# A local-attention and FFN stack on one core: the remainders of x on GpSimd, the maxima ahead of the FFN's gates, the rotary sines and the softmax division in one VectorE operation each

## The reference

```python
def attn_layer(x, Wqkv, qs, ksc, Wo):          # 16 heads of 64, windows of 32 tokens
    q, k, v = split(x @ Wqkv)
    q = l2norm(q) * qs;  k = l2norm(k) * ksc
    q = q * cos * scale + rotate_half(q) * sin * scale
    k = k * cos / scale + rotate_half(k) * sin / scale
    out = local_attention(q, k, v)             # own window and the one before it, softmax
    return out @ Wo

def ffn_layer(x, g, bln, W1, b1, W2, b2):
    xn = (x - mean(x)) / sqrt(var(x) + 1e-05) * g + bln
    a, gate = split(xn @ W1 + b1)
    return a * gelu(gate) @ W2 + b2

for i in range(6):
    x = attn_layer(shift_tokens(x), ...) + x
    x = ffn_layer(shift_tokens(x), ...) + x
```

## Time and profile before

| what | value |
|---|---|
| time, median of 3 runs | 3898.07 us (3895.68 to 3901.53) |
| the profiled execution's own time | 3892.5 us |
| its span in the trace | 3890.7 us |
| PE busy | 3564.2 us, 92% |
| DVE busy | 3275.5 us, 84% |
| POOL busy | 2781.9 us, 72% |
| ACT busy | 2617.8 us, 67% |
| mean granted clock of PE | 0.986 of full |
| DMA engines, mean busy over the span, queue of the data | 28.8% |

### The profile page before, as it was taken

The page is one execution under the profiler, slowest core; times in us unless marked ns, Lnnn a source line. Parts: engine busy times, 40 slices in busy tenths (PEclk is TensorE's granted clock), DMA queues, the critical chain, the costliest instruction groups (busy, mean ns, idle before and its releaser), DMA issues. The chain is left out here.

```text
span 3890.7 us, 104815 instructions
## 1 busy us (share of the span) xinstructions
PE 3564.2 (92%) x38876; PEld 2641.0 (68%) x38876; DVE 3275.5 (84%) x4930; ACT 2617.8 (67%) x3817; POOL 2781.9 (72%) x2428
## 2 busy tenths in 40 slices
PE   5888889699999999999999999999999999999995
PEld 4666666476777776776767676767676767777772
DVE  5656665499999999998999999999899999999993
ACT  3555555377777777777777777777777777777773
POOL 2444443288888787878787878788888888787871
PEclk9999999899999999999999999999999999999997
DMA  1122221232324232233332343222432324232221
GB/s 49 71 81 80 93 75 44 70 79 65 69 64 116 65 72 65 65 87 94 70 69 64 70 111 72 65 65 66 112 74 64 69 64 115 65 72 65 65 66 54
DMA packets 181947, 285.96 MB, mean 73 GB/s; under 512 B 52222, under 2 KB 71804, under 8 KB 175612
## 3 DMA queue, kind: packets, MB, share of 16 engines
q1 hardware_dynamic: 181884, 285.14, 28.8%
HBM read 51.11 MB, written 32.51 MB: 21 GB/s over the span
## 5 line engine op out<-in xcount | busy, mean ns | idle before, releaser
L442 PE MATMUL st_ps<-st_wqkv,st_xs 128*128 128x512 f32 x4608 | 1266.6, 410 | 47.2 <-issue 20.1
L828 POOL TENSOR_TENSOR st_qk_rot<-st_qk_rot,st_qk_sq 128x1024 f32<-128x1024 f32 x384 | 913.7, 2385 | 506.0 <-DVE st_qk_sq L728 506.0
L442 PEld LDWEIGHTS st_ps<-st_wqkv,st_xs 128*128 128x128 f32 x4608 | 811.8, 189 | 285.0 <-issue 143.5
L848 POOL TENSOR_TENSOR st_qk_rot<-st_qk_rot,st_rn 128x1024 f32<-128x1024 f32 x384 | 731.5, 1926 | 15.0
L710 DVE TENSOR_REDUCE st_nt<-st_qk_sq 128x16 f32<-128x1024 f32 x384 | 466.0, 1214 | 66.1 <-ACT st_qk_sq L559 50.1
L728 DVE TENSOR_TENSOR st_qk_sq<-st_ps,st_rot 128x512 f32<-128x512 f32 x768 | 490.5, 679 | 0.0
L714 DVE TENSOR_TENSOR st_qk_rot<-st_ps,st_rot 128x1024 f32<-128x1024 f32 x384 | 468.7, 1220 | 7.5 <-PE st_ps L457 1.6
L1525 DVE TENSOR_REDUCE at_nmx<-at_s 128x1 f32<-128x512 f32 (+3 forms) x512 | 237.0, 487 | 246.1 <-PE at_s L1138 244.8
L457 PE MATMUL st_ps<-consts_sb,st_qk_rot 128*128 128x128 f32 x3072 | 402.2, 274 | 28.9 <-POOL st_qk_rot L848 24.6
L457 PEld LDWEIGHTS st_ps<-consts_sb,st_qk_rot 128*128 128x128 f32 x3072 | 352.4, 141 | 106.5 <-issue 67.9
L877 POOL TENSOR_TENSOR st_s<-st_s,st_mx 128x512 f32<-128x512 f32 x384 | 403.6, 1071 | 10.2 <-DVE st_mx L783 9.8
(11 more groups left out here) (149 smaller groups left out, 6167.7 us busy)
## 6 DMA issues: line engine op xcount, KB each, us to landing
st_v_win<-st_v_tok SPq DMA_DIRECT2D x3072, 64.0 KB, 2.0
st_wqkv<-wqkv_parts SPq DMA_DIRECT2D x24, 1024.0 KB, 7.1
wqkv_parts<-at_w_parts SPq DMA_DIRECT2D x12, 1024.0 KB, 4.4
wqkv_parts<-at_fold_parts SPq DMA_DIRECT2D x12, 1024.0 KB, 4.7
at_w_raw<-in_wqkv SPq DMA_DIRECT2D x18, 512.0 KB, 5.5
at_wo_l<-in_wo SPq DMA_DIRECT2D x6, 512.0 KB, 5.8
rotary_tables<-at_rot SPq DMA_DIRECT2D x6, 512.0 KB, 4.7
st_rot<-rotary_tables SPq DMA_DIRECT2D x24, 128.0 KB, 2.5
```

The source lines that it names most:

```text
L442: last = pe.matmul(out[:, c * 512:(c + 1) * 512], xs[:, x_part, t * P:(t + 1) * P], wqkv[:, PROJ.index(kind), w_part, c * 512:(c + 1) * 51 ...
L828: pool.tensor_tensor(qk_rot[:, cols], qk_rot[:, cols], qk_sq[:, cols], ALU.add).then_inc(rot_done[a], 1)
L848: pool.tensor_tensor(view, view, rn[:, par, heads_of(a)].unsqueeze(2).to_broadcast([P, HEADS, DH]), ALU.mult).then_inc(normed[a], 1)
```

## The change

Four edits, all in `local_stack`:

- `remainder_half` for the running stack moves from VectorE to GpSimd. The second half of the running unit moves from the end of VectorE's tile 0 to the start of GpSimd's tile 1, ahead of the FFN's five operations. The first half of the next unit moves from VectorE's tile 2 to the start of GpSimd's tile 3. The two remainders before unit 0 stay on VectorE.
- In tile 1 the maxima of the scores stand in front of `gate(0)` and `gate(1)` on VectorE, where they stood between `gate(1)` and `gate(2)`.
- The multiplication by the sines is one operation of 1024 elements for q and one for k. It reads the halves of each head in reversed order, by a step of -32 elements.
- The division is one operation of 1024 elements. For it the inverse sums are written twice each, so `reciprocal` has 32 elements where it had 16.

```diff
-                            for g in range(2):
-                                sines = rot[:, t, 1, a * DH + g * (DH // 2):a * DH + (g + 1) * (DH // 2)]
-                                last = dve.tensor_tensor(dst[:, :, g, :], src[:, :, 1 - g, :],
-                                                         sines.unsqueeze(1).to_broadcast([P, HEADS, DH // 2]), ALU.mult)
-                            last.then_inc(rot_read[a], 1)
+                            sines = rot[:, t, 1, a * DH:(a + 1) * DH].rearrange("p (g d) -> p g d", g=2)
+                            dve.tensor_tensor(dst, src[:, :, ::-1, :], sines.unsqueeze(1).to_broadcast([P, HEADS, 2, DH // 2]),
+                                              ALU.mult).then_inc(rot_read[a], 1)
...
-                            dve.reciprocal(den[:, t2 % 2, 1, :], den[:, t2 % 2, 0, :]).then_inc(den_ready, 1)
+                            dve.reciprocal(rden[:, t2 % 2, :].rearrange("p (b s h) -> p b s h", b=2, s=2),
+                                           den[:, t2 % 2, :].rearrange("p (b h) -> p b h", b=2).unsqueeze(2)
+                                           .to_broadcast([P, 2, 2, HEADS // 2])).then_inc(den_ready, 1)
                             dve.wait_ge(den_ready, 2 * (n - 2))
-                            for b in range(2):
-                                last = dve.tensor_tensor(bank_of(s[:, t2 % 2, :], b), bank_of(weights, b),
-                                                         per_head(den[:, t2 % 2, 1, :], b), ALU.mult)
-                            last.then_inc(taken["ex"], 1)
-                        if t == 1 and alive(u, -2):
-                            gate(0)
-                            gate(1)
+                            dve.tensor_tensor(s[:, t2 % 2, :].rearrange("p (x k) -> p x k", k=WIN),
+                                              weights.rearrange("p (x k) -> p x k", k=WIN),
+                                              rden[:, t2 % 2, :].unsqueeze(2).to_broadcast([P, 2 * HEADS, WIN]),
+                                              ALU.mult).then_inc(taken["ex"], 1)
...
                             last.then_inc(max_ready, 1)
-                        if t == 2 and alive(u, 1):
-                            remainder_half(u, 1, 0)
                         if t == 1 and alive(u, -2):
+                            gate(0)
+                            gate(1)
                             gate(2)
...
-                        if t == 0 and alive(u, 0) and alive(u, -1):
-                            remainder_half(u, 0, 1)
...
             @block.gpsimd
             def _(pool):
+
+                def remainder_half(u, d, half):
+
+                    pool.wait_ge(xs_high, halves_done(u, d, half))
+                    cols = slice(half * 2 * P, (half + 1) * 2 * P)
+                    pool.tensor_tensor(xs[:, 1, cols], columns_of(batch_of(u, d), half * 2 * P, 2 * P),
+                                       xs[:, 0, cols].bitcast(F32), ALU.subtract).then_inc(xs_ready, 1)
...
+                        if t == 1 and alive(u, 0) and alive(u, -1):
+                            remainder_half(u, 0, 1)
+                        if t == 3 and alive(u, 1):
+                            remainder_half(u, 1, 0)
                         if t == 1 and alive(u, -2):
```

More of the change, by code:

```diff
@@ L249, in local_stack @@
         mx = sb("mx", [P, 2, HEADS])
-        den = sb("den", [P, 2, 2, HEADS])
+        den = sb("den", [P, 2, HEADS])
+        rden = sb("rden", [P, 2, 2 * HEADS])
         probT = sb("probT", [P, INNER])
@@ L759, in unit @@
                             for b in range(2):
-                                last = dve.tensor_reduce(den[:, t2 % 2, 0, b * 8:b * 8 + 8], heads_first(weights, b), AX.XY, ALU.add)
+                                last = dve.tensor_reduce(den[:, t2 % 2, b * 8:b * 8 + 8], heads_first(weights, b), AX.XY, ALU.add)
                             last.then_inc(den_ready, 1)
                             dve.wait_ge(den_ready, 2 * (n - 2) - 1)
-                            dve.reciprocal(den[:, t2 % 2, 1, :], den[:, t2 % 2, 0, :]).then_inc(den_ready, 1)
+                            dve.reciprocal(rden[:, t2 % 2, :].rearrange("p (b s h) -> p b s h", b=2, s=2),
+                                           den[:, t2 % 2, :].rearrange("p (b h) -> p b h", b=2).unsqueeze(2)
+                                           .to_broadcast([P, 2, 2, HEADS // 2])).then_inc(den_ready, 1)
                             dve.wait_ge(den_ready, 2 * (n - 2))
-                            for b in range(2):
-                                last = dve.tensor_tensor(bank_of(s[:, t2 % 2, :], b), bank_of(weights, b),
-                                                         per_head(den[:, t2 % 2, 1, :], b), ALU.mult)
-                            last.then_inc(taken["ex"], 1)
-                        if t == 1 and alive(u, -2):
-                            gate(0)
-                            gate(1)
+                            dve.tensor_tensor(s[:, t2 % 2, :].rearrange("p (x k) -> p x k", k=WIN),
+                                              weights.rearrange("p (x k) -> p x k", k=WIN),
+                                              rden[:, t2 % 2, :].unsqueeze(2).to_broadcast([P, 2 * HEADS, WIN]),
+                                              ALU.mult).then_inc(taken["ex"], 1)
                         if t == 3 and alive(u, -1):
```

## The result

| | before | after |
|---|---|---|
| time, median (lowest to highest) | 3897.5 us (3895.68 to 3901.53), 4 runs | 3864.12 us (3860.27 to 3868.4), 4 runs |
| ratio, 95% interval | 1 | 0.9909 [0.9895, 0.9923] |
| profiled execution, its span | 3892.5, 3890.7 us | 3860.27, 3858.5 us |
| DVE, POOL, PE busy | 3275.5, 2781.9, 3564.2 us | 3148.2, 2824.5, 3565.7 us |

The changed kernel is 0.9% faster, 33 us by the medians. The forecast was 3858 us in a range of 3842 to 3882.

What follows compares the result with a forecast made beforehand. PE was taken as nearly the bound, with waits before `pt` and `h` to win. 0.73 + 0.06 + 0.07 + 0.06 = 0.92 us a unit, 42 us over 46 units, taken as 40: 3858 us, range 3842 to 3882.

Steps and rivals of the forecast that it cites:

- The bound: Loop: PE nearly the bound at 95% busy; the chain from `q` to `pt` sets time in three of four tiles.
- Tile 1 at `pt`: Tile 1: L710 starts 0.68 us earlier without L681, merged sines save 0.06; `pt` moves forward 0.74 us.
- Tile 1 at `h`: Tile 1, FFN's `h`: L626 waits for the later of GpSimd's chain and ACT, coming 0.73 us earlier.
- Tile 2: Tile 2: `pt` gains the merged sines' 0.06 us; moving the maxima is worth 0.
- Tile 3: Tile 3: 0.07 us from the remainder no longer holding L795, plus 0.06 us from the sines.
- The changes of layer: Units that also wait for weights may give less: 40 us taken in place of 42.
- The slower rival: L728's reversed PSUM read is dear: with d = 0.5 us, +1.6 us a unit, 3970 us; chance 0.07.
- The rival with the whole fixed part: Each merged operation saves 0.14 us, 0.08 more, at four places: 0.3 us a unit, 3843 us; chance 0.07.
- The slower engine: Remainder goes to GpSimd, slower at it: 0.73 us by the line, against VectorE held 1.98 us there.
- The rival in which GpSimd is late in tile 1: Tile 1: remainder costs 1.04 us, unit gains 0.58, 3871 us; L721 missing a gap too, 3885; chance 0.15.
- Division and maxima: Division with reciprocal about 0 together; maxima worth 0, covered in tile 2 by L710's wait for the squares.
- The other signs: Expected: reciprocal 0.35 us, L877 2.06, tile 1's `pt` wait 0.2, L626 within 0.1 of GpSimd, unit 62.9 us.

Runs made afterwards that it cites:

- the two experiments that moved `h` alone: Changed kernel with GpSimd's tile 1 remainder behind the FFN's five operations: ratio to before 0.9881; changed kernel with an extra unused subtraction ahead of that remainder: 0.9985.
- the remainders alone: Kernel before with one edit, both remainders on GpSimd at the starts of its tiles 1 and 3: ratio 0.9952, median 3879.33 us.
- the remainder behind the FFN: Changed kernel with GpSimd's remainder of tile 1 behind the FFN's five operations instead of ahead: ratio to before 0.9881, median 3851.75 us.
- the sines alone: Kernel before with one edit, the sines in one operation for q and one for k: ratio 0.9966, median 3883.52 us.
- the division alone: Kernel before with one edit, division in one operation and reciprocal on 32 elements: ratio 0.9995, median 3898.4 us.
- the maxima alone: Kernel before with one edit, the maxima of tile 1 ahead of the gates: ratio 0.9997, median 3898.55 us.
- the second execution of the changed kernel: The changed kernel, unaltered, run again for direct comparison on one chip: ratio to before 0.9921, median 3866.31 us.
- twice: Changed kernel with an extra, unused subtraction of the same size ahead of GpSimd's remainder in tile 1: ratio to before 0.9985, median 3895.92 us.

## Why the prediction was right

**The bound** was read rightly. PE's waits before `pt` and `h` were what could be won, and the two experiments that moved `h` alone moved the unit by the same amount, 0.43 us one way and 0.64 the other. The time came out 6 us above the forecast, since the unit gained 0.73 us in the mean and not 0.92. Below, a tile's numbers are those of the unit shown.

**Tile 1 at `pt`.** Forecast 0.74 us, measured 15.06 - 14.32 = 0.74; the remainders alone gave 0.68. The wait is 0.29 rather than 0.22.

**Tile 1 at `h`.** Forecast 0.73, measured 21.64 - 21.06 = 0.58. GpSimd's chain ended 19.74 us after tile 0's `pt`, and the forecast's 2160.37 is 19.75 after it. That the two agree is luck, for two terms were off and cancel: L884 (before, L877) starts 0.06 us earlier after tile 0's `pt` than it did (10.99 against 11.05), not 0.16, and the remainder moves what follows by 0.59, not 0.70. What was mis-sized is the step from there to ACT: I let L626 start 0.05 us after GpSimd's end, and it starts 0.20 after it, here and with the remainder behind the FFN. That is the 0.15. In the units with the longer remainder, which moves what follows by the forecast's 0.70, `h` gains 0.48 only, and the mean over all is 0.52. L721 was forecast to end near 2157.8, 17.2 after `pt` of tile 0; as L722 it ended at 2144.35, 17.16 after it.

**Tile 2** gave 0.06 more, as forecast (34.08 - 33.44 = 0.64 in all). **Tile 3** was to give 0.07 by the missing remainder and 0.06 by the sines, and gave 0.07 together. The first of these did not come, and the reading behind it was wrong. L793, once L795, waits for `zt` with nothing ahead of it, 0.62 us; the rows are `zt` before, `zt` after and L793:

```profile
2183.73 0.27 PE L451 MATMUL st_ps<-consts_sb,st_z_tok 128*128 128x128 f32 x1
2169.65 0.27 PE L452 MATMUL st_ps<-consts_sb,st_z_tok 128*128 128x128 f32 x1
2170.07 0.59 DVE L793 TENSOR_TENSOR xT_sb<-st_ps,xT_sb 64x128 f32 x2 [0.62 <-PE st_ps L452]
```

It starts 0.15 us after `zt` ends (2169.92 to 2170.07). Before, L795 started 0.15 us after `zt` ended as well (2184.00 to 2184.15), so it was `zt`, and not the remainder ahead of it, that held it.

**Between tile 3 and the next tile 0** came 0.07 that was not forecast. `tq` there waited for GpSimd's L848, and started 0.11 us after the end of the matmuls before it (2198.00 + 1.65 = 2199.65, `tq` at 2199.76); after, these times are 2185.54 and 2185.55, and the gap is gone. It is the sines that bring it: from tile 3's `pt` to the next tile 0's it is 14.01 us before and 14.00 with the remainders alone, 13.95 with the sines alone and 13.94 after, in the mean of the steady units. That it goes by GpSimd's operation, which comes sooner by the merged sines ahead of it, is argued. The sum is 0.78 us in this unit (63.77 - 62.99) and 0.73 in the mean, where 0.92 was forecast.

**The changes of layer.** I allowed 2 us for the five units in which PE waits for new weights. In the first of them, the kernel before:

```profile
1246.87 1.63 PE L442 MATMUL st_ps<-st_wqkv,st_xs 128*128 128x512 f32 x6 [1.27 <-DMA st_wqkv<-wqkv_parts]
...
1257.15 1.14 DVE L681 TENSOR_TENSOR st_xs<-xT_sb,st_xs 128x256 fp32r<-128x256 f32 x1
...
1262.70 1.06 PE L462 MATMUL st_ps<-consts_sb,st_s 128*128 128x128 f32 x8 [0.88 <-issue]
```

and the changed kernel:

```profile
1242.73 1.63 PE L443 MATMUL st_ps<-st_wqkv,st_xs 128*128 128x512 f32 x6 [1.41 <-DMA st_wqkv<-wqkv_parts]
...
1258.49 1.06 PE L463 MATMUL st_ps<-consts_sb,st_s 128*128 128x128 f32 x8 [0.81 <-issue]
```

The wait for weights is the same, 1.3 to 1.4 us, but before, the engines behind used it to catch up: VectorE's remainder cost 1.14 us and not 1.98 there, `pt` of tile 1 came 14.37 us after tile 0's and not 15.06, and `h` 20.72 and not 21.64. After, there is less to catch up: `pt` comes at 14.30 in place of 14.32, `h` at 20.65 in place of 21.06 to 21.16. (PE's own wait before `pt`, 0.88 and 0.81, is no measure of this, as PE's `tq` ahead of it doesn't wait for GpSimd in such a unit.) From `h` to `h`, a unit with a change of layer took 0.56 us more than another before (mean of five 64.33, against 63.77), and takes 1.02 more after (64.05 against 63.03). By these two traces that is 2.3 us of the gain given back, near the 2 allowed. The size is uncertain: the kernels with the division alone and the maxima alone, whose steady unit is that of before, took 0.72 and 0.91 more there, the second execution of the changed kernel 1.12. With the remainder behind the FFN it is 2.02, partly by a longer wait for weights (1.52 us in the mean, against 1.28) and partly because `h` there comes at 21.10 in four of the five, where it otherwise comes at 20.67.

From the first `h` to the last, the changed kernel gains 39 x 0.733 = 28.6 us in the steady units, 5 x (64.33 - 64.05) = 1.4 at the changes of layer and 1.9 in the last three units, 31.9 in all. The second stage shrank by 31.7 and the span by 32.2.

**The slower rival**, a dear read with a negative step, fell: L728 takes 1.208 to 1.219 us in all 192 pairs, as the forward read L714 does. (The prediction's 1.04 ns an element is 1.07 by the earlier trace rows, (1.23 - 0.68) / 512; nothing hangs on it.) The rival with the whole fixed part fell with the sines alone. The Trainium skill (VectorE: DVE Perf Modes, The TRN2 errata) has the durations right: (1024 + 151) / 0.96 = 1224 ns by it, 1.21 to 1.22 in the rows; but in the queue the next operation starts 0.07 to 0.08 us before the end of the one before, so what a merge saves is 0.06 us and not the whole fixed part.

**The slower engine:** the remainder takes 0.64 us on GpSimd and 0.418 on VectorE at best, so GpSimd is the slower one, and the edit gains all the same, since VectorE's took 1.98 in that place.

**The rival in which GpSimd is late in tile 1** was at 0.15 and did not come as stated: the remainder took less than its 1.04 us, and L722 ended where it was forecast. But GpSimd's chain is the late one, and the forecast itself had it so, by 0.2 us over ACT's own work. ACT waits for it in all 36 units of 1000 to 3600 us without a change of layer, and that costs `h` 0.4 us, as the run with the remainder behind the FFN shows. What the prediction did not ask is whether the remainder had to stand there.

**Division and maxima** are worth nothing measurable, as forecast; of the maxima's cover, the wait for the squares, the exchange of some 20 us between the two waits above is the evidence.

**The other signs.** The reciprocal at 0.35 us, L884 at 2.06 in every tile (L877 took 2.24 before in tile 1) and tile 1's wait before `pt` came as named. L627 starts 0.20 us after GpSimd, not within 0.1, and the steady unit is 63.0 us, not 62.9. VectorE's clamp L722 waits no longer than before: in tile 1 of the steady units it takes 0.74 to 0.89 us in place of 0.92, in the others 0.33 in both kernels.

## What to carry to other kernels

When work moves from a busy engine to another, put it behind what other engines wait for there; the same remainder costs 0.3% of the time ahead of GpSimd's FFN chain, and nothing that shows behind it. Of a merge, take from the trace what lies from start to start of the instructions, not their durations. And where a unit has a wait for something from outside (weights), ask what the change saves there: the engine that was late used it to catch up, and what was won elsewhere is partly paid back in it. To see effects of 0.3% and less, take the mean of the steady units in one trace: two executions agreed within 0.03 us in 63, where the times of a kernel scatter by 8 us and more.

## What the runs showed of the hardware

- A subtraction of 128x256 with both inputs in SBUF takes VectorE 0.418 us where GpSimd does nothing, and up to 2.00 us in the loop (0.74 and 1.98 in the earlier trace rows), by where GpSimd's operations lie. On GpSimd it takes 0.63 to 0.75 us, 0.64 in the median. The Trainium skill (SBUF — State Buffer, Who interferes with whom) says that such an instruction and a GpSimd operation that reads SBUF contend for a read interface; the trace agrees, with the 0.418 and the 2.00 us.
- VectorE's instruction of 32 elements with one input in SBUF, L721 or L722, waits likewise: it takes 0.17 us at best, and 0.92 before and 0.76 after in tile 1, where it ends 0.05 us after one of GpSimd's operations (2158.67 after 2158.62 in the earlier trace rows).
- From GpSimd's end to ACT's start are 0.20 us, in the changed kernel and in those with the remainder behind the FFN and twice. From ACT's end to VectorE's it was 0.03.
- A negative step inside a read of PSUM, between runs of 32 elements, costs nothing that shows at 1024 elements: 1.208 to 1.219 us, and 1.21 to 1.23 for the forward reads.
- The reciprocal is 6.25 ns an element for 8, 16 and 32 elements alike, on top of 153 ns.
- Second stages of two executions of the same program differed by 0.3 us of 2925 while the first starts differed by 4.5 us; of this pair the difference is in the first stage. PE's wait for new weights, five times a kernel, is what scatters in the second, 1.1 to 2.1 us.
